# Four chained layers on one core: the slots of the banded attention dealt out anew, and a bias vector reordered by the matmul engine

## The reference, cut to what matters

```python
x = x + _L0_xattn_ref(_layernorm(x), ctx, ...)      # banded attention, 8 heads of 8, |q-k| <= 64
x = x + _L0_ffn_ref(_layernorm(x), ...)             # FFN on the top half of the rows by score
x = x + _L1_xattn_ref(_layernorm(x), ctx, ctx, ...) # grouped attention, 32 heads, 8 key groups
x = x + _L1_ffn_ref(_layernorm(x), ...)             # squared-relu FFN + routed product + layernorm
```

```python
x = transpose(mask, (0, 2, 1))                      # attention over the 256 columns
q, k, v = split(x @ w_in.T + b_in, 3)
scores = einsum('bqhd,bkhd->bhqk', q, k) / sqrt(d)
attn = softmax(where(|i - j| <= 64, scores, min))
o = einsum('bhqk,bkhd->bqhd', attn, v) @ w_out.T + b_out
y = relu(transpose(o)) * encodings
out = einsum('nit,io->not', y, w_ct) + b_ct
```

## Time and profile before

| | |
|---|---|
| time, median of 3 runs | 354.66 us (354.41 to 356.05) |
| the profiled execution's own time | 355.69 us |
| its span, first to last instruction | 353.9 us |
| busy in that span: PE, DVE, ACT, POOL | 318.3, 235.3, 200.3, 182.4 us |
| first scores product of the attention | 18.21 us |
| first up product of the FFN | 172.3 us |
| TensorE clock granted, mean | 0.982 |

### The profile page before, as it was taken

How to read it: one execution, slowest core, us unless ns; L and a number is a source line. 1 busy time by engine, 2 the same in 40 slices (tenths; PEclk the granted TensorE clock), 3 DMA queues, 4 the chain that set the end, 5 groups by cost and what they waited for, 6 DMA issues and landing times.

```text
span 353.9 us, 7395 instructions
## 1 busy us (share of the span) xinstructions
PE 318.3 (90%) x2258; PEld 252.4 (71%) x2258; DVE 235.3 (66%) x914; ACT 200.3 (57%) x415; POOL 182.4 (52%) x294
## 2 busy tenths in 40 slices
PE   0458999989999999999999999899999999999993
PEld 0437687767776777776686788677787768888882
DVE  2688989888979797976214535575578746761364
ACT  2446787868778777767740522467677964213210
POOL 5374947674848574758604711425063623344743
PEclk9967999999999999999999999999999999999998
DMA  6997010101010010100000000000000000010010
GB/s 192 366 373 273 3 47 1 46 3 40 8 25 22 20 30 14 34 3 3 3 0 0 2 0 0 0 2 2 1 3 0 2 2 0 0 32 15 1 44 32
DMA packets 13042, 14.53 MB, mean 41 GB/s; under 512 B 2508, under 2 KB 11724, under 8 KB 13004
## 3 DMA queue, kind: packets, MB, share of 16 engines
q1 hardware_dynamic: 12560, 13.72, 12.1%
q10 hardware_dynamic: 444, 0.33, 0.3%
HBM read 10.64 MB, written 1.05 MB: 33 GB/s over the span
## 4 chain that ended last, share of the span: by engine, by line
PE 63%; DVE 20%; issue 7%; POOL 3%; ACT 3%; DMA 2%; ACTq 1%; POOLq 0%; DVEq 0%
DVE masked L1157 7%; PE S L683 6%; PE S L356 6%; PE O L394 5%; PE ST L378 4%; PE ST L707 4%; PE S L489 4%; PE S L625 2%; PE S L553 2%; PE PJ L466 2%; PE PJ L596 2%; PE PJ L325 2%; PE O L640 2%; PE XB L614 2%; DVE st L1113 2%
## 5 line engine op out<-in xcount | busy, mean ns | idle before, releaser
L1157 DVE CUSTOM_DVE_ANT_0 masked<-S,band 128x192 bf16<-128x192 f32 x256 | 79.1, 353 | 16.2 <-PE S L356 15.4
L801 ACT ACTIVATE ex<-ST 128x384 f32<-128x384 f32 x128 | 62.4, 491 | 17.1 <-PE ST L378 16.4
L356 PE MATMUL S<-qk 128*128 128x384 f32 x128 | 53.9, 426 | 6.0 <-DVE mw L1157 3.4
L971 POOL TENSOR_SCALAR rstd<-mv 128x1 f32<-128x1 f32 x40 | 11.9, 297 | 82.8 <-DVE mv L1115 82.6
L378 PE MATMUL ST<-qk 128*128 128x192 f32 x256 | 49.0, 273 | 0.0
L378 PEld LDWEIGHTS ST<-qk 128*128 128x128 f32 x256 | 44.7, 189 | 2.0 <-issue 1.5
L356 PEld LDWEIGHTS S<-qk 128*128 128x128 f32 x128 | 24.9, 196 | 19.5 <-issue 11.8
L394 PE MATMUL O<-ex,v 128*32 128x192 f32 x512 | 34.2, 338 | 0.0
L1288 DVE TENSOR_REDUCE mw<-S 128x8 f32<-128x512 f32 x32 | 22.0, 687 | 17.9 <-PE S L553 17.9
L769 ACT ACTIVATE hs<-PJ,sb,part 128x512 fp32r<-128x512 f32 x29 | 22.5, 777 | 17.1 <-PE PJ L326 16.7
L325 PE MATMUL PJ<-xs,w0h 128*128 128x256 f32 x58 | 18.7, 342 | 14.9 <-DVE xs L1222 14.7
(11 more groups left out here) (184 smaller groups left out, 741.7 us busy)
## 6 DMA issues: line engine op xcount, KB each, us to landing
qk<-kp SPq DMA_DIRECT2D x48, 48.0 KB
w<-in_w SPq DMA_DIRECT2D x2, 1024.0 KB, 9.7
cx<-in_cx SPq DMA_DIRECT2D x1, 1024.0 KB, 8.0
cxT<-in_cxT SPq DMA_DIRECT2D x1, 1024.0 KB, 9.5
up<-in_up SPq DMA_DIRECT2D x1, 1024.0 KB, 11.3
down<-in_down SPq DMA_DIRECT2D x1, 1024.0 KB, 10.9
out<-x SPq DMA_DIRECT2D x8, 128.0 KB, 1.7
x<-in_x SPq DMA_DIRECT2D x1, 768.0 KB, 6.4
```

The source lines that it names most:

```text
L356: mm(out, r32(qp[:, t % 2, g, b, P * c:P * c + P]), r32(mv_), start=True, stop=True).then_inc(s["pe_s"], 1)
L801: A(ex[:, (n // 2) % 4, 2 * w:2 * w + 2, :], ST[n % 2][:, 0:2 * WIN].rearrange("p (h k) -> p h k", h=2), ACT.Exp, scale=SCALE).then_inc(s[ ...
L1157: last = V.tensor_tensor_reduce(out=masked[:, n % 2, h, :], in0=S[n % 2][:, WIN * h:WIN * h + WIN], in1=band[:, c, :], scale=1.0, scalar=N ...
```

## The change

1. The products of probabilities and values move from odd slots (with units 17 and 16 slots old) to even ones (18 and 17 slots old).
2. Nearly all other steps of a tile get new slots, on all engines together: projections 3, 6, 9, 12 become 3, 7, 11, 13 and their sums on DVE 4, 8, 12, 15; the values move from slot 15 of the tile before to slot 5 of their own; the way out is spread over slots 15 to 14 of the next tile, the FFN's norm and selection come half a tile later or more. The transposes of the maxima go to the end of their slot.
3. The drain of the attention grows by 8 slots: one down product a slot, in place of two, and the steps of the last tile lie among them.
4. At the start the bias comes in one piece, with `kmask`, beside `cols` in one tile `given`; ACT copies `ident` with its columns reordered (`turn`) and one product by PE puts bias, masks and `cols` into the order by heads. DVE copies the result out (`byhead`), which replaces the tables made from `ident`, and makes the low part of the weights ahead of the normalisation.
5. For tile 0 the projections come in the order keys 0, queries 0, keys 1, queries 1, in other banks.

The diff, cut to its core:

```diff
-ST_LAG, PV_LAG = 11, 16
+ST_LAG, PV_LAG = 11, 17
...
+        turn = hT[:, 2, 0:96]
...
-        PROJ = {3: 0, 6: 1, 9: 2, 12: 3}
+        PROJ = {3: 0, 7: 1, 11: 2, 13: 3}
+        MIX = {4: 0, 8: 1, 12: 2, 15: 3}
...
+        OUT = {15: (1, 0), 3: (2, 1)}
+        RATIO = {0: 0, 5: 1}
...
-            if FC <= n < 2 * FC:
-                return "down", n - FC
-            if 2 * FC + 7 <= n < 2 * FC + 11:
-                return "scatter", n - 2 * FC - 7
+            if FC + 1 <= n < 3 * FC + 1:
+                return "down", n - FC - 1
+            if 3 * FC + 2 <= n < 3 * FC + 6:
+                return "scatter", n - 3 * FC - 2
...  (PE)
-                for t, r in ((place(T_, l, PV_LAG + 1), place(T_, l, PV_LAG)) if l % 2 else ()):
+                for t, r in ((place(T_, l, PV_LAG + 1), place(T_, l, PV_LAG)) if l % 2 == 0 else ()):
...
-                if l == 2 and 0 <= t < TILES:
+                if l == 11 and 0 <= t < TILES:
                     pe.wait_ge(s["f_sc"], t + 1)
...
-                if l == 6 and 0 <= t < TILES:
+                if l == 15 and 0 <= t < TILES:
                     pe.wait_ge(s["f_sel"], t + 1)
...
-                    if l == 15:
-                        values(T_ + 1)
-                if (T_, l) == (TILES + 2, 1):
+                if l == 5 and 0 <= T_ < TILES:
+                    values(T_)
...
+                if (T_, l) == (TILES + 2, 6):
                     keys1(0)
-                if (T_, l) == (TILES + 2, 7):
+                if (T_, l) == (TILES + 2, 10):
                     values1(0)
...
+            pe.wait_ge(s["ld_first"], 32)
+            pe.wait_ge(s["ld_b0"], 32)
+            pe.wait_ge(s["act_part"], 1)
+            mm(MT[0:96, 0:12], turn, given[:, :], start=True, stop=True).then_inc(s["pe_part"], 1)
...  (ACT)
-            for j in range(4):
-                load(b0[24 * j:24 * j + 24, :], a["b0"].rearrange("(r j d) n -> j r d n", r=4, j=4)[j, 0:3], "ld_b0")
-            load(b0[96:128, :], a["b0"][96:128, :], "ld_b0")
+            load(given[:, 0:4], a["b0"], "ld_b0")
+            load(kmask, a["kmask"], "ld_b0")
...  (DVE, ahead of its slots)
+            dve.wait_ge(s["pe_part"], 1)
+            V.tensor_copy(byhead[0:96, :], MT[0:96, 0:12])
+            V.tensor_copy(byhead[96:128, :], given[96:128, :]).then_inc(s["dve_part"], 1)
+            dve.wait_ge(s["dve_part"], 1)
+            for n in range(4):
+                last = V.tensor_tensor(sb0[:, n:n + 1], b0[:, n:n + 1], part0[:, n // 2:n // 2 + 1], ALU.mult)
```

More of the change, by code:

```diff
@@ L177, in proj_bank, with order @@
         def proj_bank(t, n):
-            return (PJ, S[1], S[0], ST[0])[n] if t == 0 else PJ
-        def value_bank(t):
-            return ST[1] if t == 0 else PJ
+            return (PJ, ST[0], S[0], ST[1])[n] if t == 0 else PJ
+        def order(t):
+            return (0, 2, 1, 3) if t == 0 else (0, 1, 2, 3)
         def x_norm(t):
@@ L278, in _ @@
             load(hT[:, 0:2, :].rearrange("p a b -> p (a b)"), a["spread"], "ld_sel")
-            late = [(b1[:, :], a["b1"]), (kmask[:, :], a["kmask"]),
+            late = [(b1[:, :], a["b1"]),
                     (w1[:, :, :], a["w1"].rearrange("(k p) f -> p k f", p=P)),
@@ L356, in slot_ @@
                     mm(out, r32(qp[:, t % 2, g, b, P * c:P * c + P]), r32(mv_), start=True, stop=True).then_inc(s["pe_s"], 1)
-                t, r = place(T_, l, 9)
-                if l % 8 == 1 and live(t, r):
-                    k = 2 * t + r // 8
-                    pe.wait_ge(s["dve_max"], UNITS * t + r + 8)
-                    if k >= 1:
-                        pe.wait_ge(s["act_mt"], k)
-                    if l == 9 and T_ >= 3:
-                        pe.wait_ge(s["fa_x"], T_ - 2)
-                    for gc in range(4):
-                        last = tr(MT[:, P * gc:P * gc + P], mw[:, (r // 8), gc, :], ident[:, :])
-                    last.then_inc(s["pe_mt"], 1)
                 t, r = place(T_, l, ST_LAG)
@@ L397, in slot_ @@
                     last.then_inc(s["pe_pv"], 1)
-                t, r = place(T_, l, 26)
-                if l % 8 == 2 and live(t, r):
-                    k = 2 * t + r // 8
+                back, b = OUT.get(l, (0, None))
+                t = T_ - back
+                if b is not None and 0 <= t < TILES:
+                    k = 2 * t + b
                     pe.wait_ge(s["act_o"], k + 1)
@@ L438, in slot_ @@
                     if l in PROJ:
-                        project(T_ + 1, PROJ[l])
-                    if l == 15:
-                        values(T_ + 1)
-                if (T_, l) == (TILES + 2, 1):
+                        project(T_ + 1, order(T_ + 1)[PROJ[l]])
+                if l == 5 and 0 <= T_ < TILES:
+                    values(T_)
+                t, r = place(T_, l, 9)
+                if l % 8 == 1 and live(t, r):
+                    k = 2 * t + r // 8
+                    pe.wait_ge(s["dve_max"], UNITS * t + r + 8)
+                    if k >= 1:
+                        pe.wait_ge(s["act_mt"], k)
+                    if l == 1 and T_ >= 4:
+                        pe.wait_ge(s["fa_x"], T_ - 3)
+                    for gc in range(4):
+                        last = tr(MT[:, P * gc:P * gc + P], mw[:, (r // 8), gc, :], ident[:, :])
+                    last.then_inc(s["pe_mt"], 1)
+                if (T_, l) == (TILES + 2, 6):
                     keys1(0)
-                if (T_, l) == (TILES + 2, 7):
+                if (T_, l) == (TILES + 2, 10):
                     values1(0)
@@ L751, in slot_ @@
                     nc.scalar.copy(xsT[:, :, 64 * t:64 * t + 64], MT[:, P:2 * P].rearrange("p (k c) -> p k c", k=2)).then_inc(s["fa_x"], 1)
-                t, r = place(T_, l, 24)
-                if l % 8 == 0 and live(t, r):
+                t, r = place(T_, l, 25)
+                if l % 8 == 1 and live(t, r):
                     k = 2 * t + r // 8
@@ L846, in _ @@
                            w0[:, :, 0:96].rearrange("p n (r j d) -> p n j r d", r=3, j=4)).then_inc(s["act_w0"], 1)
+            act.wait_ge(s["ld_ident"], 16)
+            nc.scalar.copy(turn.rearrange("p (j r d) -> p j r d", j=4, r=3),
+                           ident[:, 0:96].rearrange("p (r j d) -> p j r d", r=3, j=4)).then_inc(s["act_part"], 1)
             for T_, l in SLOTS_ALL:
@@ L1160, in slot_ @@
                     last.then_inc(s["dve_max"], 1)
-                t, r = place(T_, l, 27)
-                if l % 8 == 3 and live(t, r):
-                    k = 2 * t + r // 8
-                    b = k % 2
+                t, b = T_ - 2, RATIO.get(l)
+                if b is not None and 0 <= t < TILES:
+                    k = 2 * t + b
                     dve.wait_ge(s["pe_ot"], k + 1)
@@ L1211, in slot_ @@
                 if 0 <= t < TILES:
[L1212 removed]
+                    if l == 7 and t >= 1:
                         if t == 1:
@@ L1227, in slot_ @@
                 t = T_ + 1
-                if l - 1 in PROJ and 0 <= t < TILES:
-                    n = PROJ[l - 1]
-                    m, g = 4 * t + n, n % 2
+                if l in MIX and 0 <= t < TILES:
+                    n = order(t)[MIX[l]]
+                    m, g = 4 * t + MIX[l], n % 2
                     dve.wait_ge(s["act_hs"], m + 1)
```

123 lines of the change are left out of this document (55 added, 68 removed).

## The result

The changed kernel takes 358.75 us (median of 4 runs, 357.81 to 359.50) against 355.15 (354.41 to 356.05) beside it: ratio 1.0099, interval 1.0057 to 1.0141. It is slower, by 3.6 us, where 344.9 was forecast. The profiled execution took 359.5 us, with a span of 357.7.

The account below looks back on a forecast made before the run. It took PE and DVE to limit the middle tiles by turns, DVE being fuller. Start -4.3, steady tiles -7.5 and drain +2.0 made -9.8 us, forecasting a median of 344.9 us from 354.66, range 340.5 to 351.

Parts of the forecast that it names:

- The start: Start: bias loaded earlier, first projection near 8.3 us, 5.0 us earlier, of which -4.3 us by tile 1's first scores.
- the fifth rival: Start: the bias load still takes 5.81 us and lands late, +2.1 us, 347.0; counted within the forecast's 0.62.
- Not all survives: Start: POOL builds first keys ahead of tile 1's norm, so the 5.0 us gain was taken as 4.3.
- my third rival: Tiles 1 and 2: key building blocks each split half once more, 1.2 us a tile, +2.4 us, 347.3; chance 0.12.
- The steady tiles: Middle tiles: new slots cut DVE's idle 2.4 us a tile to 1.0; -7.5 us, including 1.7 from two earlier tiles.
- PE needs some 15.7 us of work per tile: Middle tiles: PE's work summed from chain prices, against DVE's 16.36 us busy in 18.80, making DVE the fuller engine.
- near or under DVE in every pair: Middle tiles: after the change PE's worst pair of slots takes 2.1 us, against DVE's mean pair of 2.05.
- The drain: Drain: -0.4 before the up products, +1.0 in them, +1.4 at the end; +2.0 us, everything later unchanged.
- The slower one: Steady tiles: PE's transpose of `O` waits for DVE's sum into `x`, 1.9 us in 7 tiles, 358.2; chance 0.06.
- The first rival: Steady tiles: ACT takes over in crowded slots, so the new slots give nothing, 352.4 us; chance 0.14.

Follow-up runs that it names:

- e5: The kernel before with only the new start (part 4 of the change), old slots and projection order kept: 351.66 us, ratio 0.9904.
- e14: Changed kernel with first tile and drain repaired, tile 1's norm early, and both split halves in one slot in all tiles: 351.12 us, ratio 0.9875.
- e9: Changed kernel with tile 0's values and tile 1's split early, and the last tile's selection ahead of the second attention's values: 353.45 us, ratio 0.9943.
- e4: Changed kernel with DVE's sum into keys and queries over half the columns from tile 2 on (output changed): 354.07 us, ratio 0.9971.
- e6: Changed kernel with eight filler products on PE in the drain, five behind the score transpose, three behind the gather: 355.79 us, ratio 1.0019.
- e8: Changed kernel with the last tile's selection ahead of the second attention's values, on all engines: 353.79 us, ratio 0.9964.

## Why the prediction was wrong

The forecast was -9.8 us, the result a loss of 3.6. Three parts of the sum failed, by 5.1, 4.3 and 4.2 us; no two of them alone would have made the change a loss.

**The start was right.** First projection 8.69 us for 8.3 forecast; -4.6 us at unit 16 in e5, for -4.3, and -3.5 in its time. The missing 0.4 us at the first projection are two GpSimd steps of the inverse deviation: 0.41 and 0.85 us, for 0.23 and 0.57 before. They now run while DVE makes the weights' low part. The late bias load, the fifth rival, did not come.

**Tiles 0 and 1, the step that was not taken.** I wrote "Not all survives" and took 0.7 us off for tile 1's norm. The other steps that the deal moves in tiles 0 and 1 stood in the sum at nothing, without a reason; from unit 0 to unit 32 4.9 us were gone. Moving the values behind the second key sum, the norm behind the first key build and the split's halves into two slots put three DVE and GpSimd steps between PE and unit 4's scores. Undoing them gave 2.9 us at unit 32 (53.23 to 50.3 in e14), the clock's part with it. The new start with the old slots has unit 32 at 47.85, so 2.5 us stay; what part of them is the lower clock, which lasted until 36.3 us in e14 and 26.2 in e5, is open. The port rule (the Trainium skill, "SBUF — State Buffer", section Who interferes with whom) was my third rival at +2.4 us and a chance of 0.12. The trace agrees with the rule: 1.23 and 2.02 us for two halves in e9, 1.12 and 0.42 once the norm was ahead. But it did not cost the 1.2 us a tile of the rival. Both halves together took 0.57 us more than before in tile 1 and 0.39 less in tile 2; what hurt more was where the halves stood. The lower clock costs at most 1.6 us of the 4.9.

**The steady tiles, a term mis-sized.** "PE needs some 15.7 us of work per tile" was the failing step. Its pace is 17.9 (e4): with DVE relieved of 1.1 us a tile, the tile shown still took 17.94. I had priced the scores at 0.17 us everywhere, but right behind products with values they take 0.37; eight times a tile that is 1.6 us, and the earlier trace rows stopped one row short of it. The other 0.6 us are small: in e4's chain the channel product takes 0.63 and one transpose of `O` 0.61, for 0.45 and 0.44. So PE was not "near or under DVE in every pair". In the tile shown the remaining idle time of DVE was 1.55 us (18.49 less 16.94) and not 1.0, and its busy time 16.94, not 16.36, the value of the last middle tile before. The sentence of the Trainium skill, "Perfetto Trace Analysis", section Identifying the Most-Contended Engine, that matmul busy is a poor measure of PE's headroom misled me here. In a tile of 18.49 us the weight loads (14.06 us) leave 4.4 us, matmul busy (17.95) leaves 0.5, and 0.5 is what e4 won. The two rows had not agreed with the sentence; they had only differed.

**The drain, a term mis-sized and one missing.** Up to the second half's up products I had +2.0 and got +3.8: -0.4 up to the first up product as forecast, +2.2 in the up and down products, where PE has no gap, for 1.0, and +2.1 for 1.4 at the end. The missing term is the clock: +2.4 us from the up products to the second attention's first scores, where I had "unchanged" (6.06 for 3.54 us in the first up products), and some 0.4 of the +2.1 in the gather. I had even forecast that PE would idle there, and priced the idle time at its own length. e6 gave back 3.0 us by filling it, e8 5.0 by an order that has less of it.

**The rivals.** The slower one named a real wait at 0.25 us of the 1.9 it needed; the result is on its side by other causes, so its 0.06 was not earned by its mechanism. The first rival, ACT, would have had to hold PE back, and ACT waits for PE. The sum of the errors, in the profiled executions: 0.2 (unit 0 at -4.1 for -4.3) + 4.9 + 4.3 + 1.8 + 2.4 = 13.6 us, the 359.5 measured less the 345.9 forecast for them.

## What to carry to other kernels

Price an engine's pace from a whole stretch in which it has no gap, as the busy time of a window that it fills, and not from a sum of the shortest pieces. When steps are dealt out anew for the steady state, walk through the first two and the last tile apart: there the same slots cost this kernel 4.9 and 3.8 us, while they gave 3.2 in between. Idle time that a change puts on PE can be paid twice, as here, once as such and once in the clock of what follows; a few fillers told the two apart. And moving one step of a tuned order alone can be worse than moving none or all: the products with values alone cost 3.7 us.

## What the runs showed of the hardware

The same up products took 3.54 us behind a PE that was busy for 5.70 of 6.31 us, and 6.06 behind one that was busy for 5.55 of 8.30, though its longest wait was 1.13 us. Eight filler products that did nothing made the whole kernel 3.0 us faster. Scores products right behind the products with values, which have 32 columns of weights, cost 0.2 us more than elsewhere (0.37 for 0.17) in both kernels; why was not tested. A split of 0.42 us took up to 2.02 beside GpSimd's key building.
